# A selective-scan and gated-FFN layer in seven token chunks (128, 192, 256, four of 368) in place of six (256, 320, four of 368)

## What is computed

```python
sa, ca, ga, sb, cb, gb = (silu(c) @ wmod).reshape(6, 1024)   # ga, gb pushed away from zero
h  = layernorm(x) * (1 + ca) + sa
xp = h @ x_proj_w.T                          # 32 columns for dt, 16 for B, 16 for C
dt = softplus(xp[:, :32] @ dt_proj_w.T + dt_proj_b)
for t in tokens:                             # state s: 1024 features x 16
    s = exp(dt[t] * A) * s + dt[t] * B[t] * h[t]
    y[t] = (s * C[t]).sum(states) + D * h[t]
x  = x + ga * y
h  = layernorm(x) * (1 + cb) + sb
gate, up = lora_matmul(h, gate_w, ...), lora_matmul(h, up_w, ...)     # 1024 -> 2752, rank 16
x  = x + gb * lora_matmul(silu(gate) * up, down_w, ...)               # 2752 -> 1024
```

## Time and profile before

| | us |
|---|---|
| median of 3 runs | 2396.12 (2391.91 to 2397.71) |
| profiled execution | 2402.57 |
| its span, first to last instruction | 2400.6 |

### The profile page before, as it was taken

The page is one execution under the profiler, slowest core; times in us unless marked ns, Lnnn a source line. Parts: engine busy times, 40 slices in busy tenths (PEclk is TensorE's granted clock), DMA queues, the critical chain, the costliest instruction groups (busy, mean ns, idle before and its releaser), DMA issues.

```text
span 2400.6 us, 34580 instructions
## 1 busy us (share of the span) xinstructions
PE 2085.1 (87%) x11700; PEld 1888.9 (79%) x11700; DVE 1446.0 (60%) x2118; ACT 1430.1 (60%) x2798; POOL 1545.0 (64%) x960
## 2 busy tenths in 40 slices
PE   6587754877778989979999989999989999999999
PEld 3243334877767888868999978999979999999998
DVE  4665676767665688755778756678757775211111
ACT  3776766767655677665676655676656565532332
POOL 1576668988867876857876857876859897100000
PEclk9798877999889999989999999999999999999999
DMA  8777634666757677656666656666658777787785
GB/s 334 259 267 229 187 122 154 230 224 227 240 177 256 201 248 238 219 195 237 198 237 226 212 188 242 194 239 225 215 189 263 257 240 267 232 279 260 252 273 197
DMA packets 156032, 547.89 MB, mean 228 GB/s; under 512 B 17104, under 2 KB 29648, under 8 KB 152784
## 3 DMA queue, kind: packets, MB, share of 16 engines
q1 hardware_dynamic: 155856, 545.68, 68.0%
HBM read 498.32 MB, written 47.30 MB: 227 GB/s over the span
## 4 chain that ended last, share of the span: by engine, by line
PE 53%; DVE 16%; ACT 13%; issue 8%; POOL 5%; DMA 4%; SPq 0%; DVEq 0%; ACTq 0%; POOLq 0%
PE FP L762 43%; DVE ring L1168 7%; PE FP L650 4%; DVE ring L1053 3%; POOL ring L1284 2%; ACT SC L831 2%; PE FP L679 2%; ACT whi L990 2%; ACT sqb L950 2%; DVE FP L1143 1%; DMA raw<-w_gu 1%; POOL y L1257 1%; PE FP L786 1%; PE FP L624 1%; PE FP L628 1%
## 5 line engine op out<-in xcount | busy, mean ns | idle before, releaser
L1284 POOL TENSOR_TENSOR ring<-ring,c_row 128x736 f32<-128x736 f32 (+2 forms) x372 | 621.6, 1671 | 350.7 <-ACT hst L848 350.2
L762 PE MATMUL FP<-xhi,whi 128*128 128x368 f32 (+2 forms) x2160 | 713.0, 330 | 106.6 <-ACT dtb L955 27.3
L831 ACT ACTIVATE SC<-dtb,aneg 128x368 f32<-128x368 f32 (+2 forms) x768 | 409.3, 544 | 529.7 <-DVE ring L1168 525.2
L762 PE MATMUL FP<-xhi,wlo 128*128 128x368 f32 (+2 forms) x2160 | 703.7, 326 | 0.0
L762 PE MATMUL FP<-xlo,whi 128*128 128x368 f32 (+2 forms) x2160 | 703.6, 326 | 0.0
L1168 DVE TENSOR_TENSOR_SCAN ring<-SC,hst,ring 128x368 f32<-128x368 f32 (+1 forms) x640 | 579.7, 947 | 6.5 <-ACT SC L831 6.5
L1257 POOL TENSOR_TENSOR y<-y,ring 128x736 f32<-128x736 f32 (+1 forms) x320 | 555.0, 1734 | 13.7
L762 PEld LDWEIGHTS FP<-xhi,whi 128*128 128x128 f32 x2160 | 422.9, 196 | 120.7 <-ACT whi L990 66.0
L990 ACT ACTIVATE whi<-raw 128x1024 fp32r<-128x1024 f32 (+2 forms) x408 | 409.1, 1009 | 145.0 <-PE FP L786 69.7
L762 PE MATMUL FP<-hhi,whi 128*128 128x368 f32 (+5 forms) x1188 | 393.1, 331 | 66.2 <-POOL hlo L1305 46.6
L762 PEld LDWEIGHTS FP<-xlo,whi 128*128 128x128 f32 x2160 | 421.9, 195 | 1.1
(11 more groups left out here) (106 smaller groups left out, 2236.4 us busy)
## 6 DMA issues: line engine op xcount, KB each, us to landing
wlo<-lo_scratch SPq DMA_DIRECT2D x249, 576.0 KB, 4.4
raw<-w_gu SPq DMA_DIRECT2D x249, 512.0 KB, 5.0
raw<-w_dn SPq DMA_DIRECT2D x107, 448.0 KB, 4.1
wlo<-lo_scratch SPq DMA_DIRECT2D x91, 448.0 KB, 3.9
raw<-w_dn SPq DMA_DIRECT2D x53, 512.0 KB, 4.5
wlo<-lo_scratch SPq DMA_DIRECT2D x51, 512.0 KB, 4.0
raw<-w_gu SPq DMA_DIRECT2D x44, 576.0 KB, 4.7
lo_scratch<-wlo SPq DMA_DIRECT2D x44, 576.0 KB, 6.4
```

What stands on the lines that cost most here:

```text
L762: last = mm(out, w, x, start=(start and k == 0 and e == 0), stop=(stop and k == n - 1 and e == 2))
L831: A(decays(c, n, a), tile_of(dtb, c, i), ACT.Exp, scale=aneg[:, i * NS + s:i * NS + s + 1]).then_inc(a_da[a], 1)
L1284: G.tensor_tensor(buf, buf, over_pair(c_of(k)), ALU.mult).then_inc(g_hc, 1)
```

## The change

The chunk list becomes 128, 192, 256 and four of 368 tokens, so that CHUNKS is 7 and all weights are passed seven times. Chunk 0's ring gets six slots of 2 x 128 in place of five of 2 x 256; they now lie at the end of the ring's memory (ring_span), not at its beginning. For chunk 1's first slots, the waits for chunk 0's buffers are worked out from the overlap of the columns: last_of_first gives the last group of chunk 0 whose buffer overlaps. Of the ring, slots 0 and 1 of chunk 1 then overlap nothing and don't wait, slots 2 and 3 wait for the sums of 63 and 64 groups (before: 62, 63, 64 and 64 for the four). Of the C rows, the first three of chunk 1 wait for 62, 64 and 1 products (before: 62, 63 and 64). All orders and the bank plan follow from CH.

```diff
--- before.py
+++ after.py
@@ -12,7 +12,7 @@
 D = 1024
 ND = D // P
 TOKENS = 2048
-CH = [256, 320, 368, 368, 368, 368]
+CH = [128, 192, 256, 368, 368, 368, 368]
 CHUNKS = len(CH)
 AT = [sum(CH[:c]) for c in range(CHUNKS)]
 TM = max(CH)
@@ -65,7 +65,7 @@
 RAW_SLOTS, HI_SLOTS, BANKS = 3, 3, 4
 AHEAD_HI, AHEAD_RAW = 2, 4
 RING, C_SLOTS = 4, 3
-RING_FIRST, C_FIRST = 5, 5
+RING_FIRST, C_FIRST = 6, 5
 
 BC0, BC1, DA0, DA1 = range(4)
 
@@ -122,6 +122,24 @@
         return k
     c, s = divmod(k - GROUPS, NS)
     return group_id(c + 1, PAIRS * s + PAIRS - 1)
+
+
+def ring_span(c, n):
+    if c == 0:
+        at = 2 * (RING * TM - RING_FIRST * CH[0] + n % RING_FIRST * CH[0])
+        return set(range(at, at + 2 * CH[0]))
+    at = n % RING * 2 * TM
+    return set(range(at, at + CH[c])) | set(range(at + TM, at + TM + CH[c]))
+
+
+def row_span(k):
+    c, _ = row_state(k)
+    at = k % C_FIRST * CH[0] if c == 0 else (k - GROUPS) % C_SLOTS * TM
+    return set() if c == 0 and k % C_FIRST + 1 == C_FIRST else set(range(at, at + CH[c]))
+
+
+def last_of_first(spans, span):
+    return max([g + 1 for g in range(GROUPS) if spans(g) & span], default=0)
 
 
 def v_time(n):
@@ -483,7 +501,7 @@
 
         def ring_of(c, n):
             if c == 0:
-                at = n % RING_FIRST * 2 * CH[0]
+                at = min(ring_span(0, n))
                 return ring[:, :, :, :].rearrange("p r a t -> p (r a t)")[:, at:at + 2 * CH[0]].rearrange("p (a t) -> p a t", a=2)
             return ring[:, n % RING, :, 0:CH[c]]
 
@@ -491,7 +509,8 @@
             if c == 0 and n >= RING_FIRST:
                 engine.wait_ge(pe_y, n - RING_FIRST + 1)
             elif c == 1 and n < RING:
-                engine.wait_ge(pe_y, min(GROUPS, GROUPS - 2 + n))
+                if last_of_first(lambda g: ring_span(0, g), ring_span(1, n)):
+                    engine.wait_ge(pe_y, last_of_first(lambda g: ring_span(0, g), ring_span(1, n)))
             elif c:
                 engine.wait_ge(g_add, group_id(c, n) - RING - GROUPS + 1)
 
@@ -835,7 +854,7 @@
                 if k >= GROUPS + C_SLOTS:
                     act.wait_ge(g_hc, last_group_of_row(k - C_SLOTS) + 1)
                 elif k >= GROUPS:
-                    act.wait_ge(g_hc, k - 2)
+                    act.wait_ge(g_hc, max(1, last_of_first(row_span, row_span(k))))
                 elif k >= C_FIRST:
                     act.wait_ge(g_hc, k - C_FIRST + 1)
                 A(c_of(k), SC[:, BC0 + k % 2, 0:CH[row_state(k)[0]]], ACT.Copy).then_inc(a_bc, 1)
```

## The result

The changed kernel takes 2610.1 us (median of 4 runs, 2603.3 to 2618.4) against 2396.9 of before: a ratio of 1.089, with a 95% interval of 1.085 to 1.093. Its profiled execution has a span of 2603.0 us, 202.4 more than before. TensorE's mean granted clock went from 0.931 to 0.885.

A forecast was written before the change was run, and what follows sets the result against it. No engine was full in the first four periods; fixed orders lengthened them, and DMA was the narrow passes' largest load. -60 + 280 + 280 + 325 - 347 - 349 = +129 us on 2402.6 gave 2531.6, median 2525; range 2445 to 2680.

The forecast's parts named there:

- its own case: Whole kernel: narrow periods with DMA as largest load, median 2525 us, bounds 2450 to 2590; chance 0.62.
- P(128 beside 192): Chunk 0's FFN beside chunk 1's scan: DMA's 228 us at 0.82 of the period, 280 us; 245 to 310.
- The first rival: Both narrow passes: TensorE binds at 0.12 us a step and clock 0.80, 320 us each, about 2605; chance 0.18.
- its test: Sign of TensorE binding: both narrow periods have TensorE at over 0.9 of them and DMA share under 0.75.
- P(192 beside 256): Chunk 1's FFN beside chunk 2's scan: DMA's 228 us again the largest load, 280 us; 245 to 310.
- P(256 beside 368): Chunk 2's FFN beside the next scan: GpSimd's 258 us at 0.80, 325 us; bounds 304 and 349.
- S(128): First stage, without FFN work, at 128 tokens: 60 us shorter than 389, loop 44 of it; bounds -96 and -35.
- The sixth slot: Chunk 0's ring: one more slot can only let products start earlier; counted within the loop's -44 us.
- The four full chunks: The four chunks of 368 and their periods (368 beside 368, twice, then 302 and 292 us) stay unchanged.
- Plain-float rate below 256 columns: Rival: narrow rounded-float matmuls fall to plain-float rate, 213 ns at 128 columns, 320 at 192; about 2925 us; chance 0.12.
- Faster: Rival: first stage -96, narrow periods at DMA floor 228 each, P(256 beside 368) at 304; about 2364 us; chance 0.05.

The follow-up runs named there:

- the kernel with 192 columns: Changed kernel, but chunk 0's FFN matmuls (128 tokens) stream 192 columns, 64 of them zeros whose results nobody reads: 2555.8 us, ratio to before 1.067.
- the runs with 224 and 208: Changed kernel's code with six chunks, 224, 352 and four of 368, or 208 and five of 368, five ring slots for chunk 0: ratios 1.0034 and 1.0040.

## Why the prediction was right, and where it was off

The direction and the range held, and the reason given for them: one more pass over the weights costs far more than a shorter first stage gives back. What sets the narrow periods was wrong. The median, 2610, is 85 us above the forecast's 2525 and outside the 2450 to 2590 of its own case, in which DMA is the largest load; it lies in 2445 to 2680 because the range also covers the rival in which TensorE binds. Of the 85 us the parts below hold 74 (+202.6 against +129). The other 12 lie between profiled executions and medians: before is 6.5 us over its median, the changed kernel's 5.3 under. By its steps:

- **P(128 beside 192), 280 forecast, 362 measured: the step that failed.** The forecast took 0.10 us a matmul at full clock and let DMA be the largest load. The bound from one-column matmuls, 0.12 us, was the right row: a 128-column step goes at 110 to 114 ns at 2.4 GHz, the same as a 192-column one, and in the kernel with 192 columns the steps with 80 weight columns take 91 ns where those with 128 take 112 (medians of the starts), so the weight load sets it. And the clock was not full: a step went at 213 ns in the median and, by all starts recorded, 0.184 on the mean; 1718 x 0.184 = 317 us, and with about 25 for the other matmuls nearly the period. The first rival had this mechanism, TensorE bound at a clock that its own waits let fall, and its test, asked of both narrow periods, is met in this one (TensorE over 0.9 of it, DMA share 0.65 or so) and not in the next (0.84 and 0.77). It had its size wrong: 0.80 was carried over from the first stage, and the stretches of this period show 0.50 to 0.70. At 192 columns the granted clock is 0.91. That the rival's 2605 comes so near to 2610 is luck: it had 320 us for each of the two periods, and they took 362 and 293. Padding gives 66 us of the 82 back; that much is the clock's. The other 16 stay at 192 columns, with their cause open.
- **P(192 beside 256), 280 forecast, 293 measured; P(256 beside 368), 325 and 337.** Near, but the reasoned cause doesn't stand for the first: the forecast divided the DMA's 228 us by 0.82, and taking 19 MB of 76 away (estimated from the code) gave 4 us. No engine is full in these periods. That the hand-overs in fixed orders set them is argued and not shown; the quotient was a good guess with a wrong name.
- **S(128), -60 forecast, -82.6 measured.** The loop went from 269 to 202 us where 225 was forecast. The forecast priced chunk 0's 128 tokens fewer and not that chunk 1's head and first groups, also in this stage, go from 320 tokens to 192. From 128 and 192 tokens with the same 192 behind them (305.7 and 330.6 us) a token of chunk 0 is worth 0.39 us; that makes 50 of the 82.6, and leaves 33 for chunk 1's 128 tokens fewer (an estimate: a line through three runs; the runs with 224 and 208 lie 9 us under it).
- **The sixth slot**: counted as part of the loop's gain; it is none.
- **The four full chunks**: as before within 2 us, but one period 6.6 us shorter, which no run explains. Periods of this shape come at 355 to 363 us in the profiles here, also in kernels that don't differ there.
- **Plain-float rate below 256 columns**: dead, though its sign, starts 213 ns apart, did appear. Here it has another cause: at 1.2 GHz a 128-column step takes 213 ns too. When the clock is up 128 columns go at 110 ns and so do 192, and by this rival 192 would be 320.
- **Faster**: all three of its terms had to go right; the first came near (-83 of -96), the other two missed by 134 and 65 us, and 33 in P(256 beside 368).

## What to carry to other kernels

Price an added pass over weights by what does not shrink with the tokens, here the weight load (110 ns a step at 2.4 GHz whether 128 or 192 columns follow), the rounding and the fixed orders; a narrower chunk saves only the rest. Ask of the narrowest matmul in a kernel not only what it costs at full clock but whether it gets the clock back after a wait, even a short one: where it doesn't, streaming columns that nobody reads can be faster. A load divided by a usual utilization may give a good number with a wrong cause; only taking the load away tells.

## What the runs showed of the hardware that was not expected

- Rounded-float matmuls of 128 columns, each behind a load of 128 weight columns, didn't raise TensorE's clock in 64 us of work without a gap (213 ns each, 0.50 granted), but kept it at 2.4 GHz for 67 us once wide ones had raised it (111 ns). During one wait of 20.5 us it dropped; in the matmuls of 192 columns that followed, at 143 us, it came back. In the changed kernel it stayed at 0.50 for 181 us of work without a gap, nearly all of it 128 columns wide, and rose in a layernorm's plain-float matmuls of 192 columns.
- The weight load sets the step where the matmul behind it is narrow: 0.21 us with 128 weight columns and 0.13 with 80 at 1.2 GHz, for the same 128 columns streamed.
- TensorE busy is not TensorE fast: in chunk 0's period it was busy 199 of 200 us (400 to 600) and did half of what it could.
- The rule of the Trainium skill, "TensorE: Matmul & The Clock Gate", What's actually happening, that activity releases the throttle, holds in the 368- and 192-column stretches and not in the 128-column ones: 64 us of them without a gap, and 181 us in the changed kernel, released nothing.
